# Even score units, another order around the router, and the router's division on GpSimd, in a transformer layer with a small mixture of experts

## The reference

```python
h = layernorm(x) * (1 + ca) + sa
# 16 heads of 8, a rotation that keeps the even columns only, causal mask
Q, K, V = (h @ W.T + b for W, b in ((Wq, bq), (Wk, bk), (Wv, bv)))
att = softmax(where(causal, rope(Q) @ rope(K).T / sqrt(8), -1e10))
x = x + ga * ((att @ V) @ Wo.T + bo)
h = layernorm(x) * (1 + cb) + sb
t = (h @ Wm + bm).reshape(-1, 16)          # 8 slices of 16 a token
w = softmax(t @ expert_emb)                # the router: 16 experts
topw, topi = top_k(w, 2)
eo = gelu(t @ W1 + b1) @ W2 + b2           # all experts, hidden size 64
comb = sum(topw * eo[topi])                # the two chosen, weighted
x = x + gb * (comb.reshape(-1, 128) @ Wo_ffn + bo_ffn)
```

## Time and profile before

| what | value |
|---|---|
| median of 3 runs | 396.37 us (394.13 to 397.07) |
| profiled execution, its own time | 393.95 us |
| its span, first to last instruction | 392.1 us |
| busy TensorE / VectorE / ScalarE / GpSimd | 341.2 / 287.0 / 256.8 / 137.2 us |
| mean granted clock of TensorE | 0.973 of full speed |

### The profile page before, as it was taken

The page is one execution under the profiler, slowest core; times in us unless marked ns, Lnnn a source line. Parts: engine busy times, 40 slices in busy tenths (PEclk is TensorE's granted clock), DMA queues, the critical chain, the costliest instruction groups (busy, mean ns, idle before and its releaser), DMA issues.

```text
span 392.1 us, 7302 instructions
## 1 busy us (share of the span) xinstructions
PE 341.2 (87%) x2668; PEld 158.2 (40%) x2668; DVE 287.0 (73%) x590; ACT 256.8 (65%) x297; POOL 137.2 (35%) x175
## 2 busy tenths in 40 slices
PE   3759688889898899988998899898898999889996
PEld 3425244445554444423654444334554323132123
DVE  5879968997789987886689687874769447963334
ACT  8570343535268878864388888855467997968981
POOL 6246217201316424752209034941213135432500
PEclk9986699999899999999999999999999999999999
DMA  7334123200016255510126255510032355715550
GB/s 245 124 68 81 39 46 54 43 1 3 4 38 99 62 136 141 171 34 2 29 68 90 70 136 135 143 38 4 29 57 25 98 137 144 122 48 138 148 137 27
DMA packets 27115, 31.53 MB, mean 80 GB/s; under 512 B 6780, under 2 KB 17788, under 8 KB 27068
## 3 DMA queue, kind: packets, MB, share of 16 engines
q1 hardware_dynamic: 23372, 28.57, 31.6%
q0 software_dynamic: 3456, 2.39, 2.9%
q10 hardware_dynamic: 252, 0.11, 0.2%
HBM read 3.57 MB, written 1.05 MB: 12 GB/s over the span
## 4 chain that ended last, share of the span: by engine, by line
PE 60%; DVE 19%; ACT 8%; issue 7%; DMA 2%; SPq 1%; POOL 1%; ACTq 0%; DVEq 0%; POOLq 0%
PE acc L1295 20%; PE misc L1295 19%; PE big L1295 18%; ACT ring L771 7%; DVE mx L1033 6%; PE misc L1317 2%; DMA block<-qk_turned 1%; SPq L492 1%; DMA xs<-in_x 1%; POOL gm L670 1%; DVE gm L1153 1%; ACT qk_turned L780 1%; DVE second L1118 1%; DVE rest L991 1%; DVE xn L977 1%
## 5 line engine op out<-in xcount | busy, mean ns | idle before, releaser
L771 ACT ACTIVATE ring<-big 128x1024 f32<-128x1024 f32 (+2 forms) x225 | 198.4, 929 | 89.5 <-PE big L1295 88.4
L1033 DVE TENSOR_REDUCE mx<-misc 128x1 f32<-128x512 f32 (+7 forms) x155 | 87.7, 587 | 24.1 <-PE misc L1295 22.1
L1295 PE MATMUL acc<-ring,cb 128*32 128x512 f32 x512 | 67.8, 604 | 1.5 <-DVE gm L1153 1.5
L1295 PE MATMUL big<-dense,block 128*128 128x512 bf16 (+7 forms) x256 | 55.6, 318 | 5.9 <-ACT ring L771 5.6
L1295 PE MATMUL big<-tstack,w1s 128*128 128x512 bf16 x192 | 55.3, 381 | 3.7 <-ACT ring L771 3.5
L1295 PE MATMUL misc<-dense,block 128*128 128x320 bf16 (+7 forms) x170 | 43.4, 316 | 8.8 <-DVE mx L1033 8.5
L1153 DVE SCALAR_TENSOR_TENSOR gm<-acc,cb,gm 128x512 f32<-128x512 f32 (+1 forms) x41 | 30.0, 733 | 24.4 <-PE acc L1295 19.4
L1295 PEld LDWEIGHTS big<-dense,block 128*128 128x128 bf16 x256 | 30.7, 148 | 30.7 <-ACT ring L771 15.8
L1295 PE MATMUL acc<-ring,vals 128*32 128x64 f32 (+7 forms) x512 | 40.1, 414 | 0.4
L1295 PEld LDWEIGHTS misc<-dense,block 128*128 128x128 bf16 x170 | 20.8, 149 | 48.1 <-DVE mx L1033 39.5
L446 POOL DMA_DIRECT2D block<-qk_turned x66 | 39.3, 601 | 1.6 <-issue 0.9
(11 more groups left out here) (163 smaller groups left out, 464.8 us busy)
## 6 DMA issues: line engine op xcount, KB each, us to landing
gm<-wT SPq DMA_DIRECT2D x64, 256.0 KB
dense<-qk SPq DMA_DIRECT2D x42, 64.0 KB
tstack<-tp SPq DMA_DIRECT2D x18, 128.0 KB, 4.4
block<-qk_turned POOLq DMA_DIRECT2D x66, 32.0 KB, 3.3
xs<-in_x SPq DMA_DIRECT2D x4, 256.0 KB, 8.3
ca<-in_pack_a SPq DMA_DIRECT2D x1, 769.0 KB, 7.6
out<-lg SPq DMA_DIRECT2D x3, 256.0 KB, 2.3
dense<-tp SPq DMA_DIRECT2D x6, 128.0 KB, 8.9
```

Source lines behind the costliest of these rows:

```text
L771: act.activation(dst, src, func, scale=scale).then_inc(s["ring_read"], 1)
L1033: dve.tensor_reduce(mx[:, g, k:k + n, blk], src, AX.X, ALU.max).then_inc(s["misc_read"], 1)
L1295: return pe.matmul(dst, lhsT, rhs, start=start, stop=stop)
```

## The change

The softmax takes five steps in place of eight blocks: block 0; 7 with 1; 6 with 2; 5 with 3; 4. Two blocks of a step share a bank and fill it, so every unit has 1024 columns, and a group has 9. `weigh` follows each step, two steps late. The ring is indexed by a running count. Maxima in the first softmax are also issued between the two banks of a unit.

`route` on VectorE no longer sums, inverts and multiplies for batches 0 to 2: `divide_by_totals` on GpSimd halves `ex` four times by sums, raises the 32 totals to -1, and multiplies `ex` by them; VectorE then multiplies the marks by that. Batch 3 keeps the old way. `stack_q` comes after it on GpSimd, and `add_bias` after `stack_k` (in the late stage after the division).

VectorE modulates the transposed rows between the two halves of `cut_rotated`. On TensorE, x1T, tokens and logits move within the softmax, `routed` moves from after two hidden units to after four (to after six in the late stage), `values` follows it in the loops, and the second `sums_out` comes after six units there. In the late stage ScalarE takes the second sum from `acc`, and a memset on VectorE moves behind the copy of the weights. `cut_weights` is on ScalarE (two copies) and GpSimd (four instructions), parts of it in the setup and after the first softmax's gates.

```diff
-LN_LINKS, ROPE_LINKS, SHIFT_LINKS, NORM_LINKS, SPLIT_LINKS, ROUTE_LINKS = 7, 4, 4, 2, 3, (0, 5, 10, 14)
+LN_LINKS, ROPE_LINKS, SHIFT_LINKS, NORM_LINKS, SPLIT_LINKS, ROUTE_LINKS = 7, 4, 4, 2, 3, (0, 5, 10, 11)
...
-SCORE_UNITS = [(s, 2 * k, 2, 1) for s in range(4) for k in range(2)] + [
-    (4, 0, GP, 2), (5, 0, GP, 2), (6, 0, GP, GP), (7, 0, GP, GP)]
+SOFT_STEPS = [(0,), (7, 1), (6, 2), (5, 3), (4,)]
+NSS = len(SOFT_STEPS)
+def banks_of(step):
+    if len(step) == 1 and T - BLK * step[0] == T // 2:
+        return [[(k + j, step[0], j * T // 2) for j in range(2)] for k in range(0, GP, 2)]
+    return [[(k, blk, sum(T - BLK * x for x in step[:j])) for j, blk in enumerate(step)] for k in range(GP)]
+SCORE_UNITS = [(i, banks_of(step)[k:k + 2]) for i, step in enumerate(SOFT_STEPS) for k in range(0, len(banks_of(step)), 2)]
 NU = len(SCORE_UNITS)
-TURN_AT, SUM_AT, ROUTE_AT = (11, 12, 13), 18, 20
+HOME = {(k, blk): (u, T * bank + at) for u, (_, banks) in enumerate(SCORE_UNITS)
+        for bank, items in enumerate(banks) for k, blk, at in items}
+TURN_AT, SUM_AT, ROUTE_AT = (8, 10, 11), 14, 15
 EARLY = 4
 SHARED = NB - 1
...
-MIDDLE = ["yT", "xT", "ao", "ue", "uo", "x1T", "tT", "lg", ("oT", 0), "wT", ("oT", 1), "v"]
+MIDDLE = ["yT", "xT", "ao", "ue", "uo", "x1T", "tT", "lg", ("oT", 0), "wT", "v", ("oT", 1)]
 for t in range(2, HALVES + 2):
     MIDDLE += ["cb0"] * (t == CB0_AT) + CHUNKS[t]
...
+            def cut_weights(k):
+                pool.wait_ge(s["b_loaded"], 16)
+                pool.wait_ge(s["w1_rounded"], k + 1)
+                less = B["keep"][:, k:k + 1].to_broadcast([P, NE * FI])
+                rounded = combT[:].rearrange("p k t -> p (k t)")
+                pool.tensor_tensor(rounded, w1p, less, ALU.mult).then_inc(s["w1_less"], 1)
+                pool.wait_ge(s["w1_less"], 2 * k + 1)
+                if k:
+                    pool.tensor_tensor(w1s[:, :], rounded, w1f, ALU.add).then_inc(s["w1_ready"], 1)
+                else:
+                    pool.tensor_tensor(w1f, rounded, w1f, ALU.add).then_inc(s["w1_less"], 1)
+            def divide_by_totals(b):
+                pool.wait_ge(s["ex_ready"], b + 1)
+                ready, n = s["ex_shared"], TT * FH
+                pool.tensor_tensor(pairs[:, :, 0:8], ex[:, :, 0:8], ex[:, :, 8:16], ALU.add).then_inc(ready, 1)
+                pool.wait_ge(ready, 6 * b + 1)
+                pool.tensor_tensor(pairs[:, :, 0:4], pairs[:, :, 0:4], pairs[:, :, 4:8], ALU.add).then_inc(ready, 1)
+                pool.wait_ge(ready, 6 * b + 2)
+                pool.tensor_tensor(pairs[:, :, 0:2], pairs[:, :, 0:2], pairs[:, :, 2:4], ALU.add).then_inc(ready, 1)
+                pool.wait_ge(ready, 6 * b + 3)
+                pool.tensor_tensor(tot[:, :], pairs[:, :, 0], pairs[:, :, 1], ALU.add).then_inc(ready, 1)
+                pool.wait_ge(ready, 6 * b + 4)
+                pool.wait_ge(s["marks"], 2 * b + 4)
+                pool.tensor_tensor(rtot[:, :], tot[:, :], marked[:, 0:1].to_broadcast([P, n]), ALU.pow).then_inc(ready, 1)
+                pool.wait_ge(ready, 6 * b + 5)
+                pool.tensor_tensor(ex[:, :, :], ex[:, :, :], rtot[:, :].unsqueeze(2).to_broadcast([P, n, NE]),
+                                   ALU.mult).then_inc(ready, 1)
             def fold_out(b, here=None):
...
                 fold_out(b + 1, here)
-                add_bias(here)
+                divide_by_totals(b)
                 stack_q(b + 2)
                 if b + 3 < NB:
                     rsqrt(2 * b + 4, 0)
                 stack_k(b + 2, b)
+                add_bias(here)
                 experts_out(b, K_BLOCKS)
             here = ("late", NB - 2)
             fold_experts(here)
             rsqrt(2 * NB - 2, 1)
...
+            def round_weights(k):
+                if k:
+                    act.wait_ge(s["w1_less"], 2)
+                else:
+                    act.wait_ge(s["w1_loaded"], 16)
+                act.copy(w1p, w1f).then_inc(s["w1_rounded"], 1)
             def take_gates():
...
-                    link(dve.tensor_reduce(tot[:, :], ex[:, :, :], AX.X, ALU.add))
-                    link(dve.reciprocal(rtot[:, :], tot[:, :]))
-                    link(dve.tensor_tensor(first[:, :, :], first[:, :, :], ex[:, :, :], ALU.mult))
+                    if b < SHARED:
+                        dve.wait_ge(s["ex_shared"], 6 * b + 6)
+                    else:
+                        dve.wait_ge(s["ex_ready"], b + 1)
+                        link(dve.tensor_reduce(tot[:, :], ex[:, :, :], AX.X, ALU.add))
+                        link(dve.reciprocal(rtot[:, :], tot[:, :]))
+                        link(dve.tensor_tensor(first[:, :, :], first[:, :, :], ex[:, :, :], ALU.mult))
                     scattered = second[:, :, :].rearrange("p (q g) c -> p q (g c)", g=2)
                     scattered = scattered.rearrange("p q (e r f) -> p q r f e", r=2, f=2)
                     for r in range(2):
+                        if b < SHARED:
+                            share = ex[:, r::2, :].rearrange("p q (f e) -> p q f e", f=2)
+                        else:
+                            share = rtot[:, r::2].unsqueeze(2).unsqueeze(3).to_broadcast([P, n // 2, 2, NE // 2])
                         ins = dve.tensor_tensor(scattered[:, :, r], first[:, r::2, :].rearrange("p q (f e) -> p q f e", f=2),
-                                          rtot[:, r::2].unsqueeze(2).unsqueeze(3).to_broadcast([P, n // 2, 2, NE // 2]), ALU.mult)
+                                                share, ALU.mult)
                     ins.then_inc(s["w_ready"], 1)
...
-                cut_rotated(b + 2)
+                cut_rotated(b + 2, 0)
                 modulate(1, hT2, here, "x1T", 2 * b + 3)
+                cut_rotated(b + 2, 1)
...
                 divide(here, b + 1, 1)
                 if b + 3 < NB:
                     normalise(xs[:, b + 3], 2 * b + 4, 0, norm_link)
-                values(here, b + 2, b)
                 experts_out(here, experts_at(b), ahead=True)
             here = ("late", NB - 2)
             turn_output(here)
-            dve.memset(dense0[96:P].rearrange("r h t -> r (h t)").bitcast(F32), BF16_ONES).then_inc(s["tail_ones"], 1)
...
             route(here)
             divide(here, NB - 1, 0)
-            take_sum(NB - 1)
+            divide(here, NB - 1, 1)
             take_weights(here)
-            divide(here, NB - 1, 1)
+            dve.memset(dense0[96:P].rearrange("r h t -> r (h t)").bitcast(F32), BF16_ONES).then_inc(s["tail_ones"], 1)
             tail = ("tail", NB - 1)
...
                     filled(ins)
-            def scores(m, phase, u):
+            def scores(m, phase, u, halfway=None):
                 g = u // NU
-                blk, k0, n, per = SCORE_UNITS[u % NU]
-                w, at = T - BLK * blk, BLK * blk
                 pe.wait_ge(s["ring_read"], phase[0] + u + 1)
-                for bk in range(n // per):
-                    dst = big[:, 2 * (u % 2) + bk, 0:per * w]
...
-                    for j in range(per):
-                        p = GP * g + k0 + per * bk + j
-                        matmul(dst[:, w * j:w * j + w], blocks(k_block_of[m], p, blk), q_dense_of[m][:, p, at:T], start=(j == 0), stop=False)
-                    diagonals = dst.rearrange("p (n w) -> p n w", w=w)[:, :, 0:BLK]
+                for bank, items in enumerate(SCORE_UNITS[u % NU][1]):
+                    dst = big[:, 2 * (u % 2) + bank, :]
+                    for j, (k, blk, at) in enumerate(items):
+                        p, w = GP * g + k, T - BLK * blk
+                        matmul(dst[:, at:at + w], blocks(k_block_of[m], p, blk), q_dense_of[m][:, p, BLK * blk:T], start=(j == 0), stop=False)
+                    n, apart = len(items), items[-1][2] or BLK
...
+                        halfway()
                 ins.then_inc(s["ring_filled"], 1)
...
-                if g == 0 and blk == 0 and m < len(LAST_IN_ACC):
+            def weigh(m, phase, g, i):
+                last = max(u for u in range(NU) if SCORE_UNITS[u][0] == i)
+                pe.wait_ge(s["ring_read"], phase[0] + g * NU + last + 1 + CREDIT["ring_read"])
+                if g == 0 and i == 0 and m < len(LAST_IN_ACC):
                     pe.wait_ge(s["misc_read"], LAST_IN_ACC[m] + 1 + CREDIT["misc_read"])
-                if blk == 0 and phase[2]:
+                if i == 0 and phase[2]:
                     pe.wait_ge(s["acc_read"], NG * m)
                     wait_taken(pe, m - 1, g - 2)
-                for k in range(GP):
-                    u = next(x for x in units if SCORE_UNITS[x][1] <= k < SCORE_UNITS[x][1] + SCORE_UNITS[x][2])
-                    at = (k - SCORE_UNITS[u][1]) * w
-                    ins = matmul(acc[VW * k:VW * k + VW, g, BLK * blk:T], vals[:, GP * g + k, blk, :],
-                                 ring[:, (g * NU + u) % RING, at:at + w], start=(blk == 0), stop=(blk == NS - 1))
+                for blk in SOFT_STEPS[i]:
```

(49 more changed lines are left out.)

116 lines of the change are left out of this document (50 added, 66 removed).

## The result

The changed kernel takes 397.72 us (median of 20 runs, 396.42 to 399.35), the kernel before in the same sessions 395.33 us (20 runs, 393.30 to 397.07). The ratio is 1.0069, with a 95% interval of 1.0050 to 1.0087: 2.7 us slower. The prediction said 405, some 9 to 11 us slower: the direction is right, the size is not.

What follows compares the result with a forecast made beforehand. The prediction took TensorE, busy 87% of the span, as the bound. +3.0 (first softmax) - 7.6 (loops) - 3.8 (late stage) - 3.0 (clock) = -11.4 us against the profiled 393.95 us gave 405 us, range 387 to 411.

Steps and rivals of the forecast that it cites:

- The power: In the division on GpSimd, raising 32 totals to -1 takes 5.5 us, between 1.1 and 6.9.
- the two rivals with a cheap power: Power on GpSimd of 1.1 us, kernel at 389 us, chance 0.27; or of 1.8 to 4.5 us, 394.5 to 400, chance 0.20.
- The filled banks: In the softmaxes, full 1024-column units gain TensorE at most its idle time, 0 to 2.4 us each; 2.0 taken.
- only if nothing later is late: Condition on the 2.0 us softmax gain: it counts only without later lateness, and the forecast expected such lateness.
- the route's earlier start of 0.9 us: In the loops, VectorE's reordered work starts the route 0.9 us earlier, bounds 0 and 1.1, at 204.3 in loop 1.
- The chain: Loop 1's division on GpSimd: exponentials at 210.0, power from 214.1 to 219.6, VectorE's waiting sum 0.7, product 1.3, weights at 222.7.
- nothing is given back: In the loops, the expert stage behind the first output is TensorE's own work, so the 3.8 us lost each stay lost.
- The block DMAs: In the loops, six query-block DMAs behind GpSimd's product land last, at 228.0, moving the first expert output to about 228.1.
- The clock: TensorE stands about 4 us in three places and then runs slower: 1.0 us lost each, 3.0 in all, bounds 0 and 6.
- The late stage: Batch 2: route starts at 290.3, weights at 308.7, third output moves from 311.98 to 315.8; 3.8 us lost.
- the first rival: The power on GpSimd costs only 1.1 us, so the kernel gains 5.2 us and takes 389; chance 0.27.
- The first softmax: Cutting expert weights off VectorE gains 3.0 us, bounds 0 and 4.0; TensorE's maxima waits fall from 4.8 to 2 or less.

Runs made afterwards that it cites:

- experiment 5: The changed kernel with GpSimd's power of 32 elements replaced by a product, so weights are not divided by their totals: 385.02 us, ratio 0.9767.
- experiment 6: The changed kernel with GpSimd's power of the totals computed twice into the same place: 413.27 us, ratio 1.0493.
- experiment 4: experiment 1's kernel with the expert weights cut on VectorE again, nothing of it on ScalarE and GpSimd: 389.14 us, ratio 0.9863.
- experiment 3: The kernel before with the division on GpSimd and ScalarE's exponential of the logits three scaled blocks earlier: 408.04 us, ratio 1.0342.
- experiment 1: The changed kernel with the division back on VectorE in every batch: 386.55 us, ratio 0.9804.
- experiment 7: The changed kernel with only the sum by halves on GpSimd, reciprocal and products on VectorE: 386.40 us, ratio 0.9803.
- experiment 8: experiment 1's kernel with GpSimd's bias addition in the loops moved to right behind xb: 386.05 us, ratio 0.9782.
- experiment 9: experiment 7's kernel with GpSimd's bias addition in the loops moved to right behind xb: 383.77 us, ratio 0.9739.
- experiment 10: The changed kernel with the reciprocal alone on VectorE in place of GpSimd's power, and the bias addition right behind xb: 385.45 us, ratio 0.9789.
- experiment 11: experiment 9's kernel with a power of the totals that nothing reads, on GpSimd between the halves and the block DMAs: 409.48 us, ratio 1.0396.
- experiment 12: experiment 11's kernel with the unread power moved behind GpSimd's block DMAs in the two loops, late stage unchanged: 384.39 us, ratio 0.9737.

## Why the prediction missed

**The power: right.** 5.5 us forecast from 1.03 us for four elements, 5.42 measured; the two rivals with a cheap power fall. Experiments 5 and 6 show that it decides, one for one beyond the first 1.2 us a stage.

**The filled banks: the first step that failed.** "TensorE can gain at most its idle time, 0 to 2.4 us a softmax", and "It counts only if nothing later is late, and below something is." The sum credits the banks and the new order with nothing in the loops but the route's earlier start of 0.9 us; the runs give them 5.4 us (experiment 4).

The bound took it that TensorE's work stays, since its columns do. From the last expert output of loop 0 to the first hidden unit of loop 1 the kernel before took 37.55 us (180.22 to 217.77) with 34.55 of work, the changed one 34.16 (179.79 to 213.95) with 33.18. That is 3.4 us shorter, 2.0 of idle time and 1.4 of work; the steps need 36 in place of 44 matmuls of the mask (`earlier_query`), 7.6 us busy in place of 9.1.

"Only if nothing later is late" is wrong too. With the division on GpSimd in both, the changed kernel is 1.0342 - 1.0069 = 10.8 us faster than experiment 3's. With it on VectorE, where no power is late, the same parts bring 7.7. Not all of the 3.4 us reaches the end: a whole loop is only 1.5 us shorter in experiment 1. In its loop 0 TensorE waits 3.5 us for maxima behind the first output in place of 2.1, and its loop 1 has the collision of experiments 7 to 9.

**The chain: the second step, 2.8 us too long in each loop.** The forecast let the power begin at 214.1; it began at 212.06. The exponentials were there at 209.25 in place of 210.0. From the first half to the power it took 2.7 us, more than the bare 1.8 but less than the 4.1 that the alternation with VectorE was given. (L1118 ends 0.55 us after xb in the rows, 210.50 against 209.95, not 0.7.) That the two engines hold each other up shows beside GpSimd's long additions (experiments 7 to 9; in the late stage of the changed kernel L1187 took 2.03 us in place of 1.06 beside the bias addition), but costs little beside the short halves (L1166 took 0.92 us in place of 0.69 there) and nothing beside the power. So "VectorE's waiting sum 0.7" fell away too, and the product took 1.06, not 1.3. Weights ready at 219.8 in place of 222.7, 2.8 us behind the route's start less than forecast. And "nothing is given back" holds in loop 1 but not in loop 0: there the first output comes 4.5 us later behind the route's start than in experiment 1, the next route 3.0, for TensorE waits less for maxima afterwards.

**The block DMAs: not last.** Issued at 218.7 and landed by 224.1, not at 228.0, because the chain ahead of them was shorter. TensorE had its own work until 225.46. But the step looked in the right place: experiment 10 has this wait at 1.3 us and experiment 11 at 11.6, where the forecast had 2.1 (226.0 to 228.1).

**The clock: a price of its own.** From the weights' transposes to the first output TensorE takes 5.6 us, and 3.1 in experiment 7, which has the same order: 225.46 - 219.84 against 216.46 - 213.34. The 2.5 us stand against 1.0 in the sum, behind 2.65 us idle and not 4. Experiment 6 shows no more for a longer stand: its 5.5 us a stage cost 5.6. A short one can cost too: in experiment 1 TensorE stood 0.99 us ahead of the transposes, was granted 0.63 behind them, and took 4.6 us to the first output, where experiment 7, behind 0.90 us, took 3.1 at full clock. Why the one fell and the other didn't, the runs don't show.

**The late stage: right in size, in part by luck.** Third output 316.35 for 315.8, 4.4 us lost for 3.8, with the weights at 307.9 for 308.7. But the route starts at 291.32 and not at 290.3, and the power begins 7.9 us behind it and not 9.8. What made up for it are the last halves beside the bias addition, and outputs at half speed:

```profile
299.19 5.43 POOL L671 TENSOR_TENSOR rtot<-tot,marked 128x32 f32<-128x32 f32 x1
305.86 2.03 DVE L1187 TENSOR_TENSOR second<-first,ex 128x256 f32<-128x256 f32 x2 [4.68 <-POOL ex L673]
308.68 1.09 PE L1365 MATMUL misc<-ident,second 128*128 128x128 f32 x4 [3.70 <-DVE y L1108]
```

From route to route the stage loses 4.1 us, against 4.8 in the sum with its clock. (A power of 1.1 us would by the forecast's own terms gain 0.6 us here, 3.8 less 4.4, where it says 1.0; the first rival's 5.2 is then 4.8.)

**The first softmax: right in size; the sign that was to show it did not come.** The cutting is worth 2.3 us, which the noise doesn't tell from the 3.0 of the sum. But the waits for the maxima, said to fall to 2 us or less, did not the earlier trace rows:

```profile
PE misc L1343 <- DVE mx L1076: 4.8, 9, 1.3
```

VectorE does 3.4 us less in that stretch and TensorE waits as long, in more pieces. The last maxima end at 99.4 us in place of 101.1, which the scatter of such positions could also give. How the 2.3 us come about stays open.

In sum, the forecast had +3.0 for the gains and -7.6 - 3.8 - 3.0 = -14.4 for the three stages, in which the earlier starts of the routes (0.9, 0.9 and 0.7) are already taken off; the runs have +7.7 for all but the division and -10.5 for it. A loop, forecast to lose 3.8 and 1.0 for the clock, lost 1.5 and 1.3. The sign came out right because the power was sized right: its 5.42 us outweigh a gain that was put far too low.

## What to carry to other kernels

When a change gains on one side of a join and loses on the other, add both: work that ends sooner lets the late chain start sooner, unless something shown in the trace holds its start. Before moving a step to another engine, list what stands behind it on that queue, DMA issues first, and what else will fill the DMA queues by then; an issue that falls behind a bulk transfer costs its delay and a slower landing on top (some 6 us each here). Split a moved computation by price: sums of halves fit on GpSimd, a 0.35 us reciprocal that becomes a 5.4 us power does not.

## What the runs showed that was not expected

- A power on GpSimd is paid by the element: 4 elements a partition 1.03 us, 32 elements 5.42. As a straight line through these two sizes that is 0.157 us an element above some 0.4, an estimate; sizes between weren't run.
- During that power VectorE's two-input operations of 512 elements ran at their usual 0.69 us, while the addition of 512 elements on GpSimd stretched one to 2.03 us.
- Small transfers (six of 32 KB) issued 1.9 us after or just ahead of the same bulk took up to 8.1 and up to 2.4 us to land.
- The first hidden unit of loop 0 lay between 124.85 and 126.90 us in the profiles of experiments 1, 7, 8, 9 and 12, which differ little up to there: about 2 us of a single profile's position are scatter.
